# Gated cross-attention block on one core: centred queries from mean rows, and the order of gates, squares and token centres

## What is computed

```python
def ln(x): m = mean(x, -1); v = var(x, -1); return (x - m) / sqrt(v + 1e-5)

def mlstm_head(q, k, v, ig, fg):                     # 8 heads of 64
    cs = concatenate([0, cumsum(log_sigmoid(fg))])
    log_D = where(tril, (cs - cs.T)[1:, 1:], -inf) + ig.T
    m = max(log_D, -1); D = exp(log_D - m)
    C = (q @ k.T / 8) * D
    n = maximum(abs(C.sum(-1)), exp(-m))
    return C / (n + 1e-6) @ v

q = ln(x); gates = concat(q, ctx, ctx) @ gate_kernels + gate_bias
x = x + tanh(g_xattn) * head_rms_norm(mlstm(q, ctx, ctx, gates))
t = quant8(ln(x))                                    # scale 127 / max|t| for each token
h = relu(t @ ternary(w_gate).T) ** 2 * (t @ ternary(w_up).T)      # 2048 wide
x = x + tanh(g_ffn) * (quant8(h) @ ternary(w_down).T)
```

## Time and profile before

| | before |
|---|---|
| median of 3 runs | 601.32 us (600.64 to 601.65) |
| profiled execution | 600.03 us, its span 598.3 us |
| PE busy | 565.5 us, 95% |
| DVE busy | 525.9 us, 88% |
| ACT busy | 452.9 us, 76% |
| POOL busy | 129.4 us, 22% |
| chain that ended last | PE 79%, ACT 8%, DVE 6% |

### The profile page before, as it was taken

How to read it: one execution, slowest core, us unless ns; L and a number is a source line. 1 busy time by engine, 2 the same in 40 slices (tenths; PEclk the granted TensorE clock), 3 DMA queues, 4 the chain that set the end, 5 groups by cost and what they waited for, 6 DMA issues and landing times.

```text
span 598.3 us, 18337 instructions
## 1 busy us (share of the span) xinstructions
PE 565.5 (95%) x6506; PEld 339.5 (57%) x6587; DVE 525.9 (88%) x1151; ACT 452.9 (76%) x926; POOL 129.4 (22%) x284
## 2 busy tenths in 40 slices
PE   8986679999999999999999999999999999999997
PEld 4744435656565655656565665656565565656454
DVE  4799898989989898998989898998989899897965
ACT  4799889686876869687786868687786868777563
POOL 3267142130301212120221213020121212021100
PEclk9999989999999999999999999999999999999999
DMA  8968050050605023050503205050502305030001
GB/s 302 383 237 300 23 175 22 28 187 3 213 0 194 18 84 127 18 193 0 199 13 140 72 31 181 0 211 0 194 18 89 122 18 194 3 107 2 19 36 36
DMA packets 44257, 62.68 MB, mean 105 GB/s; under 512 B 1864, under 2 KB 25920, under 8 KB 44224
## 3 DMA queue, kind: packets, MB, share of 16 engines
q1 hardware_dynamic: 44224, 62.24, 29.5%
HBM read 53.72 MB, written 8.51 MB: 104 GB/s over the span
## 4 chain that ended last, share of the span: by engine, by line
PE 79%; ACT 8%; DVE 6%; issue 5%; POOL 1%; DMA 1%; SPq 0%; DVEq 0%; ACTq 0%; POOLq 0%
PE gb L1226 16%; PE ub L1226 16%; PE yb L1252 16%; PE tp L1273 8%; PE ab L1260 7%; PE ab L1240 4%; PE tp L1300 3%; PE ab L1283 3%; PE ab L1261 2%; ACT wdT L531 1%; ACT wgT L539 1%; POOL stage L449 1%; PE ab L1334 1%; ACT relu L549 1%; DVE stage L816 1%
## 5 line engine op out<-in xcount | busy, mean ns | idle before, releaser
L1226 PE MATMUL gb<-wgT,xqT 128*128 128x512 bf16 x486 | 126.9, 381 | 4.0 <-issue 3.9
L1226 PE MATMUL ub<-wuT,xqT 128*128 128x512 bf16 x492 | 127.2, 380 | 1.6 <-DVE stage L816 0.3
L1252 PE MATMUL yb<-wdT,stage 128*128 128x512 bf16 x466 | 112.0, 383 | 6.7 <-ACT stage L561 3.4
L547 ACT ACTIVATE relu<-gb 128x512 f32<-128x512 f32 x128 | 75.2, 587 | 46.0 <-PE gb L1226 45.6
L816 DVE TENSOR_TENSOR stage<-relu,ub 128x512 f32<-128x512 f32 x128 | 86.8, 678 | 15.7 <-ACT relu L549 15.5
L1226 PEld LDWEIGHTS ub<-wuT,xqT 128*128 128x128 bf16 x512 | 49.2, 98 | 62.6 <-DVE stage L816 4.7
L549 ACT ACTIVATE relu<-relu 128x512 f32<-128x512 f32 x128 | 80.7, 631 | 4.1
L943 DVE SCALAR_TENSOR_TENSOR dmat<-ab,dmat 128x384 f32<-128x384 f32 x128 | 65.1, 549 | 18.7 <-POOL dmat L457 13.0
L1252 PEld LDWEIGHTS yb<-wdT,stage 128*128 128x128 bf16 x496 | 45.9, 98 | 50.7 <-ACT stage L561 3.5
L1226 PEld LDWEIGHTS gb<-wgT,xqT 128*128 128x128 bf16 x512 | 45.9, 100 | 45.0 <-issue 1.0
L457 POOL TENSOR_SCALAR_AFFINE_SELECT dmat<-dmat 128x256 f32<-128x256 f32 x128 | 55.5, 461 | 58.8 <-ACT dmat L607 46.7
(11 more groups left out here) (139 smaller groups left out, 899.5 us busy)
## 6 DMA issues: line engine op xcount, KB each, us to landing
dmat<-max_rows SPq DMA_DIRECT2D x15, 1024.0 KB, 5.0
values<-in_ctx_v SPq DMA_DIRECT2D x16, 520.0 KB, 7.6
xs<-in_x SPq DMA_DIRECT2D x16, 512.0 KB, 5.8
cT<-in_ctx_t SPq DMA_DIRECT2D x16, 512.0 KB, 6.8
out<-stage SPq DMA_DIRECT2D x31, 256.0 KB, 2.0
stage<-in_w_gate SPq DMA_DIRECT2D x4, 1024.0 KB, 13.0
stage<-in_w_up SPq DMA_DIRECT2D x4, 1024.0 KB, 13.4
stage<-in_w_down SPq DMA_DIRECT2D x4, 1024.0 KB, 6.6
```

The costliest lines, as they stand in the source:

```text
L547: nc.scalar.activation(relu[:, c % 2, :], gb[c % 2][:, :], ACT.Relu).then_inc(g_free, 1)
L1226: last = nc.tensor.matmul(bank[c % 2][:, :], xqT[par][:, t, d, :], w[:, d, c * CH:(c + 1) * CH], start=(d == 0), stop=(d == KD - 1))
L1252: done = nc.tensor.matmul(yb[:, :], hqT[:, c, :], wdT[:, c, :], start=(c == 0), stop=(c == KF - 1))
```

## The change

1. **Queries.** From batch 3 on, `x` is also loaded transposed (`x_t`, laid out on the host) straight into `qT`. Only the mean has to be taken off: PE turns the column of means into rows that all 128 partitions hold (`mean_rows`, two transposes into `yb`), and DVE subtracts them in place (`centre_queries`, two `tensor_tensor`). `attention_norm`, `q_columns` and ACT's copies are left to batches 0 to 2. The queries then lack the factor `rstd`. The head norm takes it out again, if the floor of the normaliser is scaled by the deviation `std`: ACT makes `std`, POOL multiplies `enm` and the 1e-6 by it (`normaliser_floor`). The gates get `rstd` in `gates_in`: the query part and the context part stand apart in PSUM, and three instructions join them. The first half of `down(b - 1, 1)` waits for the centred queries, since it writes the bank that the mean rows were in.
2. **Order on DVE.** `gates_in` goes ahead of `head_squares`, whose second half goes behind `log_forget`.
3. **Tokens.** From batch 2 on ACT makes the centres (`token_centres`, negated, with the sign taken back in the scale), after its copy of the hidden rows, which now comes ahead of `tokens_rstd`. DVE does `hidden(b, 1, 1)` ahead of the maxima.
4. **Ahead of the loop.** The dummies ahead of `weight_total(1)` are 19 in place of 6.

```diff
+            def turned(n, par):
+                sp.dma_start(qT[par][:, :, :], x_t[bass.ds(n, 1), :, :].rearrange("o (k p) s -> p (o k) s", p=P)).then_inc(xt_in[par], 16)
...
                 queries(n, par)
+                if not at(n, 2):
+                    turned(n, par)
                 keys(n, par)
...
+            def normaliser_floor(n, npar):
+                gp.wait_ge(std_ready, n - 1)
+                gp.wait_ge(enm_ready, n + 1)
+                spread = std[npar][:, :, None].to_broadcast([P, T, NH])
+                nc.gpsimd.tensor_tensor(enm[npar][:, :, :], enm[npar][:, :, :], spread, ALU.mult).then_inc(floor_ready, 1)
+                nc.gpsimd.tensor_scalar(floor_eps[:, :], std[npar][:, :], NORM_EPS, 0.0, ALU.mult, ALU.add).then_inc(floor_ready, 1)
...
+            def token_centres(n, npar):
+                act.wait_ge(ln2_step, LN2_K * n + 4)
+                for t in range(T):
+                    nc.scalar.activation(xm[:, t, :], x2[npar][:, t, :], ACT.Identity, scale=-1.0,
+                                         bias=mv2[:, t, 0:1]).then_inc(centred, 1)
...
-                if m is None:
-                    hidden_cols(b, 0)
-                if n is not None:
-                    tokens_rstd(n)
-                if m is not None:
-                    hidden_cols(b, 0)
+                hidden_cols(b, 0)
+                if n is not None:
+                    if not third:
+                        token_centres(n, npar)
+                    tokens_rstd(n)
...
+            def centre_queries(m, par):
+                dve.wait_ge(rows_full, m - 2)
+                dve.wait_ge(xt_in[par], turned_loads(m, par))
+                for t in range(T):
+                    half = qT[par][:, :, t * P:(t + 1) * P]
+                    mean_row = yb[:, None, t * P:(t + 1) * P].to_broadcast([P, KD, P])
+                    nc.vector.tensor_tensor(half, half, mean_row, ALU.subtract).then_inc(q_ready, 1)
...
             def gates_in(m):
                 dve.wait_ge(tp_full, FULL * (gate_use(m, GATES) + 1))
+                if at(m, 0, 1, 2):
...
+                else:
...
+                    for t in range(T):
+                        nc.vector.scalar_tensor_tensor(gates[:, t, :], of_queries[:, t, :], rstd[:, t:t + 1], gbias[:, t, :],
+                                                       ALU.mult, ALU.add).then_inc(gate_scaled, 1)
+                    dve.wait_ge(gate_scaled, T * (m - 2))
+                    nc.vector.tensor_tensor(gates[:, :, :], gates[:, :, :], of_context, ALU.add).then_inc(tp_free, 1)
...
                 hidden(b, 0, 1)
+                if prev and m is not None:
+                    centre_queries(m, par)
...
-                if m is not None:
+                if not prev:
                     attention_norm(m, par)
...
+            def mean_rows(b, m):
+                pe.wait_ge(stat_step, STAT_K * (m + 1))
+                pe.wait_ge(o_ready, 2 * b - 1)
+                for t in range(T):
+                    last = nc.tensor.transpose(yb[:, t * P:(t + 1) * P], mv[:, t, 0:1].to_broadcast([P, P]), ident[:, :])
+                last.then_inc(rows_full, 1)
...
-            keep_warm(6, ub[1])
+            keep_warm(19, ub[1])
             weight_total(1)
...
                 chunk(b, 0, 2, par)
+                if prev and m is not None:
+                    mean_rows(b, m)
...
-                if m is not None:
+                if not prev:
                     q_columns(m, par)
                 if prev:
-                    down(b - 1, 1, 0, KF // 2)
+                    down(b - 1, 1, 0, KF // 2, m)
```

More of the change, by code:

```diff
@@ L30, with gated_block @@
 GATE_TILES = 4
-def gated_block(nc, x, ctx_t, ctx_v, small_in, w_gate, w_up, w_down, max_rows, out):
+def gated_block(nc, x, x_t, ctx_t, ctx_v, small_in, w_gate, w_up, w_down, max_rows, out):
     B, S, D = x.shape
@@ L93, in gated_block @@
         rstd = sb("rstd", [P, T], F32)
+        std = [sb(f"std{i}", [P, T], F32) for i in range(2)]
+        floor_eps = sb("floor_eps", [P, T], F32)
         q = sb("q", [P, T, D], F32)
@@ L176, in gated_block @@
         x_in = [sem(f"x_in{i}") for i in range(2)]
+        xt_in = [sem(f"xt_in{i}") for i in range(2)]
         ct_in = [sem(f"ct_in{i}") for i in range(2)]
@@ L182, in gated_block @@
         q_ready = sem("q_ready")
+        rows_full = sem("rows_full")
+        std_ready = sem("std_ready")
+        gate_scaled = sem("gate_scaled")
+        floor_ready = sem("floor_ready")
+        centred = sem("centred")
+        centred_here = sem("centred_here")
         tp_full = sem("tp_full")
@@ L733, in step @@
                     squares(n)
-                if m is not None:
+                if third:
                     for t in range(T):
@@ L1241, in hidden_transposes, with down @@
                     last.then_inc(a_full[e], 1)
-            def down(b, t, first, last):
+            def down(b, t, first, last, m=None):
                 for c in range(first, last):
@@ L1247, in down @@
                         pe.wait_ge(o_ready, 2 * b + t)
+                    if c == 0 and m is not None:
+                        pe.wait_ge(q_ready, Q_K * (m + 1))
                     if c % (KF // 2) == 0:
@@ L1284, in q_columns @@
                     last.then_inc(a_full[t], 1)
+            def mean_rows(b, m):
+                pe.wait_ge(stat_step, STAT_K * (m + 1))
+                pe.wait_ge(o_ready, 2 * b - 1)
+                alone(pe, pe_passed)
+                for t in range(T):
+                    last = nc.tensor.transpose(yb[:, t * P:(t + 1) * P], mv[:, t, 0:1].to_broadcast([P, P]), ident[:, :])
+                last.then_inc(rows_full, 1)
             def gate_products(m, par, first, last, tiles=GATE_TILES):
@@ L1294, in gate_products @@
                             pe.wait_ge(ct_in[par], loads_of(m, par))
+                        elif at(m, 0, 1, 2):
+                            pe.wait_ge(a_free[t], column_use(m) + 1)
                         else:
-                            pe.wait_ge(a_free[t], column_use(m) + 1)
+                            pe.wait_ge(q_ready, Q_K * m + t + 1)
                     src, row = (cT[par], KD + kd) if part == 0 else (qT[par], kd)
                     width = P // tiles
+                    whole = at(m, 0, 1, 2)
+                    col = t if whole else T * part + t
                     for g in range(tiles):
-                        done = nc.tensor.matmul(tp[width * g:width * (g + 1), t * 2 * NH:(t + 1) * 2 * NH],
+                        done = nc.tensor.matmul(tp[width * g:width * (g + 1), col * 2 * NH:(col + 1) * 2 * NH],
                                                 src[:, kd, t * P + width * g:t * P + width * (g + 1)], gk[:, row, :],
-                                                start=(part == 0 and kd == 0), stop=(part == 1 and kd == KD - 1))
+                                                start=(kd == 0 and not (whole and part == 1)),
+                                                stop=(kd == KD - 1 and not (whole and part == 0)))
                         if j == T * 2 * KD - 1:
@@ L1475, in _ @@
                 done.then_inc(y_full, 1)
-_INS = ["x", "ctx_t", "ctx_v", "small", "w_gate", "w_up", "w_down"]
+_INS = ["x", "x_t", "ctx_t", "ctx_v", "small", "w_gate", "w_up", "w_down"]
 def kernel(**inputs):
```

112 lines of the change are left out of this document (70 added, 42 removed).

## The result

The changed kernel takes 617.97 us (median of 4 runs, 617.79 to 618.46) where the kernel before, beside it, takes 600.98: a ratio of 1.0283, 95% interval 1.0265 to 1.0300. It is slower, by 17 us; the forecast was 613.5 in a range of 600 to 618. The profiled execution has a span of 616.3 us (598.3 before).

What follows compares the result with a forecast made beforehand. PE, busy 95%, was taken as the bound, with DVE hand-overs nearly closed. From the profiled 600.03 us, +11.0 (13 steps), -0.1 (step 14) and +2.0 (ahead) gave 612.9, or 614.2 from the median; 613.5 was taken, range 600 to 618.

Steps and rivals of the forecast that it cites:

- PE's own work: PE in each step: eight transposes of `q` removed (1.2 us), two for mean rows added (0.3): net -0.9 us.
- First hand-over: Centring on DVE between mean rows and scores: head 7 waits for head 5's weighing, +0.4 us a step (0.1 to 0.6).
- Second hand-over: Gate sums to `a`: DVE needs 4.8 us against PE's cover of 3.8; PE waits 1.0 us a step (0.7 to 1.3).
- Third: From `a` through `hidden(b, 1, 0)` to `ub` of `chunk(b, 1, 2)`: PE waits, +0.4 us a step (0.2 to 0.5).
- Sum of a step: One loop step: -0.9 + 0.4 + 1.0 + 0.4 = +0.9 us, unrounded +0.85; thirteen steps +11.0 us.
- Token centres: Centres moved from DVE to ACT, beside ACT's idle time; PE doesn't wait for the tokens: 0 us.
- Ahead of the loop: Thirteen more dummies delay `weight_total(1)` and ACT's `wuT`, which busy ACT can't make good: +2.0 us (0.5 to 2.3).
- PE stays the bound: Rival: `a` comes in time, each of 13 steps gains the full 0.9 us, 591 us in all; chance 17%.
- only the wait for `a` stands: Rival: centring hides in DVE's idle time, the wait at `ub` is absorbed; 603 to 605 us; chance 10%.
- The clock falls in the loop: Rival: waits bring a lower-clock stretch into each step, 1.3 us more, 13 times: 630 us; chance 3%.

Runs made afterwards that it cites:

- the two runs: Changed kernel with 6 dummies in place of 19: 615.84 us; kernel before with 19 in place of 6: 602.85 us.
- The last trace: Changed kernel with 6 dummies, early mean rows, second squares behind the gates, `a` ahead of the scalings, `hidden(b, 1, 0)` ahead of the running maximum: 601.14 us.
- the two combinations: Changed kernel with 6 dummies, squares ahead of gates, mean rows ahead of the chunk: 616.32 us with `hidden(b, 1, 0)` also early, 602.32 without that move.

## Why the prediction was right, and where it was short

**Sign and mechanism.** The kernel is slower because hand-overs that were nearly closed opened. By the places named it went as forecast: PE idle ahead of the transposes of `a`, `ub` behind it released by `hidden`, DVE idle ahead of the centring, the first chunk at 45 us. The median lies at the upper edge of the range, 4.5 us over the forecast, and two of its four executions lie above 618: that the size is still within the range is luck. The steps, 35.24 and 35.43, are over the 34.9 to 35.0 that were to show it.

**PE's own work, -0.9.** Right within 0.1: the transposes gave 1.21. The mean rows take 0.31 from start to start (349.39 to 349.70), but only 0.21 of it is new: the scores start 1.17 us behind `ub` now (348.53 to 349.70) and started 0.96 behind it before (337.21 to 338.17).

**First hand-over, +0.4.** The mechanism holds, the size was too large. The mean rows and the wait together are +0.48 in the table where 0.7 stood in the forecast. DVE starts to centre 0.42 us behind the start of the mean rows, not 0.6; the centring itself takes 0.60 a half, as taken (349.81 to 351.01 for two). Less the 0.21 of the mean rows that is 0.27 for the wait, where the forecast had 0.4; the run with the mean rows ahead of the chunk puts it at 0.22.

**Second hand-over, +1.0: the term that was mis-sized.** It measured +1.44 (0.23 ahead of the cumulative sum, 1.21 ahead of `a`). From the second half of `down` to the transposes of `a` there are 5.24 us on PE, against the cover of 3.80: 0.31 until DVE's first gate instruction, 4.87 to the end of `a`, 0.06 to PE. The forecast had 0.15 and 4.66. So DVE saw the sums later by 0.16, its chain was longer by 0.21, and 0.06 was left out. The 0.21 stand ahead of ACT's pair: `nabs` comes 0.63 behind the first gate instruction, not 0.53, and the second `zz` 2.35 behind it, not 2.16. From there to `scl` it is 0.80, and the forecast had 0.78. The cumulative sum's own wait for the logarithm was not seen: the forecast said that the new order serves it.

**Third, +0.4.** Right in every other step (+0.38), short by 0.13 in the rest (+0.53).

**Sum of a step.** +1.18 measured, +0.85 forecast. The profiled execution took 618.06 us against the 612.9 of the sum, 5.1 over: 12 x 0.33 = 4.0 by the steps, 1.5 by the first one of the loop (below), and 0.4 less by the last. The run of the old kernel with the new order alone measures the second and third terms by themselves, 0.92 + 0.43, and the forecast had 1.0 + 0.4. What the forecast took for a sum of independent terms is not one, though. That order alone costs 17.4 us in the old kernel and 11.0 in the new one, and the new kernel with the old order is still 5.9 us above the kernel before, of which 2.1 are the dummies. With the squares first PE's saving of 0.9 goes into its wait for the logarithm: PE comes to it earlier, DVE does not.

**Token centres, 0.** Right for the loop that the forecast looked at, and shown there by the run of the old kernel. In the changed loop, which DVE's hand-overs set, they gain 0.15 a step, and in the last step 0.5, where I had put 0.1.

**Ahead of the loop, +2.0.** Right: 2.1 and 2.3 in the two runs. Not foreseen was the first step of the loop, 2.3 longer and not 0.85. By the timelines 0.8 of it stand at its beginning, where the second half of the token transposes waits 1.03 us for ACT's `xq` in place of 0.23; the rest is the step's usual growth with a longer wait ahead of `ub`, 0.85 us. In the old kernel with the new order the `xq` wait is 0.35, so that part needs more of the change than the order. Which part is not settled.

**The rivals.** "PE stays the bound" and "only the wait for `a` stands" are refuted, the latter by the run with the early `a`: the wait only moves. "The clock falls in the loop" did not come about. In the changed kernel, columns as in rows 2:

```profile
200.00:400.00 200.00, 188.10 (x2317) 111.72 (x2344) 176.93 (x397) 150.40 (x327) 38.53 (x97) 1.00 0.29 99
```

The granted clock is 1.00, the 2.4 GHz level, with PE busy 188 of 200 us and single waits of about 1 us. The Trainium skill (TensorE: Matmul & The Clock Gate, What's actually happening) takes the throttled state for the default and activity for what releases it. By that rule the trace agrees as far as this: waits of this length in a loop do not bring the lower clock back. The longest that a run here has in each step, those ahead of `ub` with `a` early (16.3 us in 13 times, up to 1.6), don't either: its granted clock from 200 to 400 us is 1.00. Longer ones in the loop no run here shows.

**A rival that was missing.** I had looked at DVE only as the end of single hand-overs. With the hand-overs of the logarithm, of `a` and ahead of `ub` in time, a step is 34.3 us and not the 33.3 of PE's own work (34.15 less 0.9, an estimate). The last trace suggests that DVE's work and its own waits for PE and ACT fill the time, so that DVE sets a pace too. That is argued from its waits and not shown by a run: 0.55 us of it are PE's wait for the statistics, which this kernel's early mean rows bring. No order tried made a gain of the 0.9 us of work taken from PE.

**What stays open.** Why every second step is 0.1 to 0.2 us longer in most of the variants and in the kernel before is not. In the changed kernel `hidden(b, 1, 0)` starts 8.26 us behind the gates in one and 8.43 in the other, and no row names a releaser. Whether the last kernel with the mean rows back behind the chunk would be faster was not tried.

## What to carry to other kernels

Before moving work, write down for each hand-over when its input is ready, when its reader wants it, and what stands between on the engine that makes it; the room (here 0.5 us ahead of `a`) is what an edit can spend, and what goes beyond it shows up in each step as long as nothing behind it has room. Work that is ahead of a wait is free, and the same work behind the wait is not: the sums of squares stood where DVE idles 1.07 us without them, and were moved onto the path. A hand-over brought forward helps only until its other input or the next one in line is late, so look at the one behind it, and try such edits one at a time. Put together, the 14 us between the two combinations hung on one such place.

## What the runs showed of the hardware that was not expected

- The time spent at the lower clock (1.2 GHz) ahead of the loop does not set the time of this kernel. It differs between executions of one and the same kernel: the four of the changed kernel have mean granted clocks of 0.997, 0.992, 0.989 and 0.994 and take 618.06, 617.79, 617.89 and 618.46 us. So the two low stretches in the profiled execution with 6 dummies, where the one with 19 has one, can't be put down to the dummies; and with the two it is 2.1 us faster.
- ACT's pair of small operations costs DVE more than its busy time: from the start of the second `zz` to `scl` are 0.80 us (363.20 to 364.00), in which ACT works two operations of 0.31 and 0.22 us. The rest is the end of `zz` itself and the crossings between the engines.
- One matmul record of the 128x128 mean row is 0.27 long, and its reader on DVE starts 0.42 us behind the start of the pair.
